# Two edits at the end of a fused RG-LRU and FFN layer: the order of LayerNorm sums and squares, and the queues of the last stores

## The reference

```python
xg = gelu(x)
# _rglru, once forward and once with the scan reversed:
xx = xg @ Wx + bx
a  = sigmoid(xx @ Wga + bga) * sigmoid(a_logit)
xin = sqrt(1 - a*a) * (sigmoid(xx @ Wgx + bgx) * xx)
h  = linear_scan(a, xin)          # h[t] = a[t]*h[t-1] + xin[t]
y  = h @ Wo + bo
# around them:
z = (y_fwd + y_bwd) / 2 + x
attn = gelu(z) @ ld_W + ld_b + x
x1 = layernorm(x + attn)          # over the 1024 features
f = clip((x1 @ sign(W).T) * scale + bias, -100, 100)
out = layernorm(x1 + f)
```

## Time and profile before

| | us |
|---|---|
| two runs, slowest core | 743.37 and 775.15, median 759.26 |
| the profiled execution, slowest core | 746.07 |
| its span on core 0, the slowest, from first to last instruction | 744.5 |
| spans of cores 1 to 7 | 729.6, 725.1, 743.0, 727.3, 735.6, 742.1, 727.0 |
| TensorE busy on core 0 | 618.0 |
| ScalarE, VectorE, GpSimd busy | 351.4, 329.8, 52.9 |
| one store of the output on SP's queue, issue to landing, median | 2.7 |
| the same on GpSimd's queue | 3.6 |

### The profile page before, as it was taken

How to read it: one execution, slowest core, us unless ns; L and a number is a source line. 1 busy time by engine, 2 the same in 40 slices (tenths; PEclk the granted TensorE clock), 3 DMA queues, 4 the chain that set the end, 5 groups by cost and what they waited for, 6 DMA issues and landing times.

```text
span 744.5 us, 7159 instructions; the slowest of 8 cores (725.1 to 744.5 us)
## 1 busy us (share of the span) xinstructions
PE 618.0 (83%) x2667; PEld 261.7 (35%) x2720; DVE 329.8 (44%) x193; ACT 351.4 (47%) x260; POOL 52.9 (7%) x100
## 2 busy tenths in 40 slices
PE   1449999999999999999999849997987879789400
PEld 0004444444444444444444314443332324224000
DVE  0000000004768767768763210212449558679553
ACT  2442322336787787787761220213364368758500
POOL 2010000000000000001132111100000000000000
PEclk9999999999999999999999988999999989979655
DMA  8996000002322322232449998715742000012142
GB/s 180 250 201 105 1 0 1 1 2 41 44 33 39 43 39 33 43 43 28 71 63 186 210 191 129 183 56 174 239 126 86 0 1 0 1 56 114 56 113 113
DMA packets 23218, 61.34 MB, mean 82 GB/s; under 512 B 2704, under 2 KB 2704, under 8 KB 23184
## 3 DMA queue, kind: packets, MB, share of 16 engines
q0 software_dynamic: 13824, 27.27, 23.6%
q1 hardware_dynamic: 8208, 29.42, 12.8%
q10 hardware_dynamic: 1152, 4.19, 2.1%
HBM read 75.55 MB, written 8.39 MB: 113 GB/s over the span
## 4 chain that ended last, share of the span: by engine, by line
PE 61%; DMA 17%; DVE 10%; issue 6%; ACT 5%; SPq 0%; DVEq 0%; POOLq 0%; ACTq 0%
PE psA L152 32%; PE psB L152 29%; DMA A<-x 6%; DMA A<-Wof 4%; DMA A<-Wob 3%; DMA out<-A 2%; DVE A L905 2%; DMA A<-Wffn 2%; DVE A L688 1%; DVE A L729 1%; DVE A L803 1%; DVE A L721 1%; ACT srbf L629 1%; DVE srbf L632 1%; DVE A L911 1%
## 5 line engine op out<-in xcount | busy, mean ns | idle before, releaser
L152 PE MATMUL psA<-A 128*128 128x512 bf16 x1503 | 356.8, 392 | 62.0 <-ACT A L329 22.4
L152 PEld LDWEIGHTS psA<-A 128*128 128x128 bf16 x1536 | 150.5, 100 | 263.0 <-issue 97.0
L152 PE MATMUL psB<-A 128*128 128x512 bf16 x1004 | 225.8, 380 | 2.8 <-DVE A L568 1.8
L152 PEld LDWEIGHTS psB<-A 128*128 128x128 bf16 x1024 | 100.3, 98 | 123.7 <-issue 3.8
L429 DVE TENSOR_SCALAR A<-A,dvec_sb 128x2048 f32<-128x2048 f32 x16 | 20.6, 1286 | 168.8 <-ACT A L425 168.8
L440 DVE TENSOR_TENSOR A<-A 128x2048 f32<-128x2048 f32 x16 | 36.7, 2292 | 51.0 <-ACT A L433 51.0
L573 ACT ACTIVATE A<-A,dvec_sb 128x1024 bf16<-128x1024 f32 x16 | 18.4, 1148 | 81.0 <-DVE A L568 81.0
L425 ACT ACTIVATE A<-psB,vecs_sb 128x2048 f32<-128x2048 f32 x16 | 31.5, 1967 | 31.9 <-PE psB L152 31.9
L431 ACT ACTIVATE A<-A 128x2048 f32<-128x2048 f32 x16 | 30.6, 1910 | 23.8 <-DVE A L429 23.8
L568 DVE SCALAR_TENSOR_TENSOR A<-psA,A 128x1024 f32<-128x1024 f32 x8 | 9.8, 1224 | 71.8 <-PE psA L152 43.2
L152 PE MATMUL psB<-A,ones_sb 128*1 128x512 bf16 x128 | 34.3, 399 | 7.0 <-DVE A L911 3.7
(11 more groups left out here) (57 smaller groups left out, 350.2 us busy)
## 6 DMA issues: line engine op xcount, KB each, us to landing
A<-x SPq DMA_DIRECT2D x40, 512.0 KB, 8.8
A<-x ACTq DMA_DIRECT2D x8, 512.0 KB, 14.9
A<-Wof POOLq DMA_DIRECT2D x16, 256.0 KB, 10.9
A<-Wob POOLq DMA_DIRECT2D x16, 256.0 KB, 12.8
A<-Wffn SPq DMA_DIRECT2D x8, 512.0 KB, 5.0
out<-A SPq DMA_DIRECT2D x8, 512.0 KB, 2.7
out<-A POOLq DMA_DIRECT2D x8, 512.0 KB, 3.6
A<-Wxf POOLq DMA_DIRECT2D x8, 256.0 KB, 32.2
```

The costliest lines, as they stand in the source:

```text
L152: inst = e.matmul(oa, lh, rh, start=st, stop=sp)
```

## The change

Two parts. In `make_ln2_apply`, the stores of half 1 go to ScalarE's queue (even chunks) and SP's queue (odd chunks) instead of SP's and GpSimd's; those of half 0 stay. In the FFN loop the statistics of a chunk are split into two entries, its sum (slot 2) and its square (slot 3). The sums stay where both were; the squares of all eight chunks are issued behind the last sum. It applies to both halves.

```diff
@@ -730,7 +730,10 @@
                 for j in range(2):
                     k = 2 * pk + j
-                    deng, q = (("sync", "dX") if k % 2 == 0 else ("gpsimd", "dG"))
+                    if h == 1:
+                        deng, q = (("scalar", "dO") if k % 2 == 0 else ("sync", "dX"))
+                    else:
+                        deng, q = (("sync", "dX") if k % 2 == 0 else ("gpsimd", "dG"))
                     bd.op(deng,
                           lambda e, k=k, j=j:
                           e.dma_start(out_hbm.ap()[k * 128:(k + 1) * 128,
@@ -869,6 +872,7 @@
         sq_ops = []
+        deferred2 = []
@@ -918,16 +922,21 @@
             if o >= 2:
                 sq_ops.pop(0)()
 
-            def _stats(o=o):
+            def _sum(o=o):
                 stats_tiles(lambda k, t: r2bf_ap8[k][:, t * 512:(t + 1) * 512],
                             r2bfB[o], o, 2)
+
+            def _sq(o=o):
                 stats_tiles(lambda k, t: rsq_ap8[k][:, t * 512:(t + 1) * 512],
                             rsqS[o], o, 3)
-            deferred.append(_stats)
+            deferred.append(_sum)
+            deferred2.append(_sq)
         flush_bg()
         while sq_ops:
             sq_ops.pop(0)()
         for f in deferred:
+            f()
+        for f in deferred2:
             f()
```

## The result

The changed kernel takes 749.18 us, the median of 24 runs; the kernel before takes 745.19 us, the median of 23. The ratio is 1.0061, with a 95% interval of 1.0045 to 1.0077: the change costs 0.6%, some 4.5 us. (A few executions of either kernel are disturbed and far longer; the ratio leaves them out, and one of them, 775.15 us, was among the two whose median, 759.26 us, was known before.)

A forecast was written before the change was run, and what follows sets the result against it. The start of L612 behind the statistics, and at the end adds alternating with stores, then GpSimd's DRAIN, set the time. 746.07 us profiled + 8.4 for the squares - 3.7 at the end = 750.8 us; range 743 to 766.

The forecast's parts named there:

- the bounds alone: Statistics of both halves: 4.0 to 11.2 us more; the upper one gives 757.3 us from the profiled run.
- Squares behind sum 7: End of each FFN half: L612 waits for 18 matmuls behind copy 7 and starts 4.2 us later.
- Two of the signs: Profile afterwards: L612 6.6 us behind copy 7's end instead of 2.4; TensorE idle before sum 6 about 2 us longer.
- my lower bound: End of each FFN half: with the squares at full clock throughout, L612 starts only 2.0 us later.
- Half 1 is as half 0: End of FFN half 1: the same 4.2 us later as in half 0, together 8.4 us.
- Rival (a): End of both FFN halves: packed squares hold full clock through the broadcasts, chunk 1 gains 3.05 us; 743.3 us, chance 0.15.
- No gain from the early sums: Row operations L605 and L609, which read only the sum: at most 0.2 us gained, counted as nothing.
- Four pairs at 4.1 us: Stores of half 1, behind the last LayerNorm: each pair still takes 4.1 us from the add's end, nothing gained.
- Rival (b): Stores of half 1: the hardware queue escapes the slow stores, core 3 becomes the slowest; 747.3 us, chance 0.1.
- The end: Block's end: GpSimd's DRAIN runs early, under the row operations, so the end comes 3.7 us sooner.
- Rival (c): Block's end: the 8.46 us of DRAIN stand behind the last landing whoever issued it; 754.5 us, chance 0.1.
- Rival (d): Both FFN halves: clock stays at half through the squares, 11.2 us more, 3.7 less at the end; 753.6 us, chance 0.15.

The follow-up runs named there:

- Fillers: The changed kernel with 18 matmuls that nobody reads between sum 5 and sum 6 of each half: 744.25 us, ratio 0.9994 to the kernel before.
- late memset: The kernel before with only half 1's store queues changed, plus a small GpSimd memset (no DMA) behind the last add: 743.56 us, ratio 0.9971.

## Why the prediction was right or wrong

**The time.** 750.8 us were predicted, 749.18 measured, within 743 to 766. Against the profiled execution the forecast was +4.7 us, or +0.63%, the measured ratio is +0.61%. What failed is the step from there to the time of the kernel before. I added +4.7 to the profiled 746.07, noted that it lay near the lower of two runs, and left their median, 759.26, standing as the kernel's time. Against that number, 750.8 forecasts a kernel that is faster by 8 us, which my sum never said; the changed kernel is 0.6% slower. 23 runs of the kernel before give 745.19, beside the profiled one; the median of two, with 775.15 as one of them, was 14 us too high. The upper end of the range, 766, hung on the same number and was far too wide: from the bounds alone it would have been 757.

**Squares behind sum 7: right in mechanism, 0.5 us short per half.** 4.2 us were forecast, 4.7 measured (4.4 to 4.8 over all cores and halves). The term that was off is the time at half clock. I took 4.9 us from the dense group at 658.06; here it was 5.6 to 5.8, which gives 0.35 to 0.45 of the 0.5. Two of the signs were off in size by it or like it: L612 came 7.1 to 7.2 us behind copy 7 and not 6.6, and TensorE's idle stretch before sum 6 grew by 2.8 us and not by about 2. The experiments show both factors: four squares instead of eight cost 2.3 us, and at full clock the eight cost 1.9, the 2.0 us of my lower bound.

**"Half 1 is as half 0": some 0.4 us less.** The shift of half 0 reaches half 1 reduced, because chunk 1's matmul group meets the rise of the clock earlier. Rival (a) named the place and the 3.05 us; with all squares deferred 0.4 of it came on most cores (0.7 on two, nothing on one), with four 1.1. The clock did not stay full through the squares, and so (a) did not happen. Fillers brought about the half of it that concerns the squares, not the other: the clock was at 0.50 again in the broadcasts. The time was then that of before, not (a)'s 743.3 (a ratio of 0.996 to the profiled 746.07).

**No gain from the early sums: right.** L605 starts 1.3 us behind copy 7's end, and L612 waits for TensorE all the same.

**Four pairs at 4.1 us: right.** Undisturbed pairs took 4.0 to 4.2 us from issue to landing, where add's end to landing was 4.1. Two hardware queues move 1.05 MB no faster than a hardware and a software queue. By the Trainium skill ("DMA: Bandwidth & Descriptors", Latency and other measured facts) I had put 1.6 us for four pairs beside it; from the first to the fourth add, three pairs, it is 19.9 to 20.2 us on undisturbed cores, where it was 20.1 to 20.2, so at most 0.3 of that shows. Rival (b) is refuted by the slow pairs on hardware queues.

**The end: right in size, in part by luck.** 3.7 us less were forecast, 3.9 measured, 5.3 to 5.5 us from the last add to the end (6.7 on core 5, whose last pair was slow) where I had written 5.5. But I took DRAIN for a wait behind the landing of GpSimd's store, and that it is only where the landing is late. Rival (c) said that it would stand behind the last landing, whoever issued it, so that nothing is gained; it didn't. It stands behind GpSimd's own last instruction, whatever that is, and took 7.7 us at the least. Both readings free the end when GpSimd's list ends early enough, and so the forecast of the time held. The late memset tells the readings apart: it kept only 1.2 us of the gain (tail 8.05 instead of 9.2), where mine would have kept all of it. What the Trainium skill says ("VectorE: DVE Perf Modes", The DRAIN you can't avoid) of DRAINs of 12 ns on all engines holds here for ScalarE (8 ns), and for GpSimd in none of the kernels.

Rival (d), half clock throughout, is refuted by the windows: the last of the squares ran at 0.98 to 0.99.

## What to carry to other kernels

Work that an engine does while it waits is free only where it stands in the queue; move it behind the late input and it costs its full time, and on TensorE more (here 4.7 us instead of 1.9), where the engine comes out of an idle stretch at half clock. Before an engine is taken off the last step, look at when its list ends and what the block's end costs it: in these kernels GpSimd has to be done some 8 us before the others, and more if its last DMA is slow. And before a number of before is believed, see how many runs stand behind it.

## What the runs showed that I had not expected

- GpSimd's DRAIN at the end of the block takes 7.7 us even 40 us after its last DMA was issued, 8.1 to 8.5 us behind a DMA of 4 or of 512 KB, and where that DMA takes over 4.4 us to land, it lasts until 3.8 to 4.0 us behind the landing.
- Eighteen matmuls that nobody reads make the changed kernel 0.7% faster (0.9994 against 1.0061 of the kernel before), by keeping the granted clock at 1.00.
- The stores of two neighbouring cores seem to slow each other on any queue: up to 6.8 us instead of 4.0 to 4.2 for a pair. With more output buffers no add waited for a pair, one of 5.3 us included.
